# Graph layers on one core: six rows of z in step in place of five, other PSUM banks, row 5 of o in phase 2

## The reference, cut to what matters

```python
# layer 0
xw = x @ weight
Vxw = adj @ xw
scale = jnp.sum(d_list * filt * d_list, axis=0)
x = _layernorm(x + adj @ (scale[:, None] * Vxw) + bias)
# layer 1
X_in = (adj / where(rowsum(adj) > 0, rowsum(adj), 1)) @ x @ W_in
X_out = (adj.T / where(rowsum(adj.T) > 0, rowsum(adj.T), 1)) @ x @ W_out
out = _layernorm(x + X_in + X_out)
```

## Time and profile before

| | |
|---|---|
| median of 3 runs | 735.02 us (734.94 to 735.05) |
| the profiled execution | 734.96 us |
| its span | 733.1 us, so 1.9 us lie around it |
| PE busy | 726.4 us, 3293 matmuls |
| DVE busy | 598.0 us |
| ACT busy | 522.6 us |
| GpSimd busy | 18.6 us |
| DMA | 222.27 MB, mean 303 GB/s |

### The profile page before, as it was taken

One profiled execution on the slowest core, in us unless ns is written; L12 is line 12 of the kernel. 1 busy time (PEld: TensorE's weight loads), 2 busy tenths in 40 slices (PEclk: granted clock), 3 DMA queues, 4 the chain that ended last, 5 costly groups with the idle time before them and its releaser, 6 DMA issues.

```text
span 733.1 us, 9244 instructions
## 1 busy us (share of the span) xinstructions
PE 726.4 (99%) x3293; PEld 600.8 (82%) x3293; DVE 598.0 (82%) x754; ACT 522.6 (71%) x1336; POOL 18.6 (3%) x15
## 2 busy tenths in 40 slices
PE   9999999999999999999999999999999999999997
PEld 5888888888888888888888888888888888888885
DVE  6898997756363888998786778997898999899996
ACT  6888888737354639467374547998989898777673
POOL 1112400000000000000000000000000000000000
PEclk9999999999999999999999999999999999999999
DMA  9999999456443677666646469999989999999991
GB/s 371 426 425 423 425 427 387 173 179 229 173 173 118 226 266 307 232 268 247 230 175 266 157 213 390 381 386 389 367 325 391 385 368 379 379 362 352 357 367 34
DMA packets 36109, 222.27 MB, mean 303 GB/s; under 512 B 3680, under 2 KB 8544, under 8 KB 9568
## 3 DMA queue, kind: packets, MB, share of 16 engines
q1 hardware_dynamic: 35792, 221.56, 78.4%
q10 hardware_dynamic: 272, 0.13, 0.1%
HBM read 219.58 MB, written 2.10 MB: 302 GB/s over the span
## 4 chain that ended last, share of the span: by engine, by line
PE 99%; DVE 0%; ACT 0%; issue 0%; DVEq 0%; ACTq 0%
PE accA L716 13%; PE accA L721 13%; PE accB L716 13%; PE accB L721 13%; PE accA L726 13%; PE accB L726 13%; PE accC L721 6%; PE accC L716 6%; PE accC L726 6%; PE nat L775 3%; PE accB L821 1%; PE nat L782 0%; DVE stats L685 0%; ACT rows L428 0%; DVE accC L590 0%
## 5 line engine op out<-in xcount | busy, mean ns | idle before, releaser
L469 DVE TENSOR_TENSOR lo<-raw,hi 128x2048 fp32r<-128x2048 f32 (+2 forms) x249 | 476.1, 1937 | 86.0 <-ACT hi L325 74.8
L325 ACT ACTIVATE hi<-raw 128x512 fp32r<-128x512 f32 x512 | 315.4, 622 | 68.8 <-DMA raw<-in_adjT_b 42.4
L716 PE MATMUL accA<-hi,x_hi 128*128 128x512 f32 x416 | 163.3, 393 | 0.1
L721 PE MATMUL accA<-hi,x_lo 128*128 128x512 f32 x416 | 161.9, 389 | 0.0
L726 PE MATMUL accA<-lo,x_hi 128*128 128x512 f32 x416 | 116.4, 389 | 0.0
L716 PE MATMUL accB<-hi,v_hi 128*128 128x512 f32 x256 | 100.0, 391 | 0.0
L721 PE MATMUL accB<-hi,v_lo 128*128 128x512 f32 x256 | 99.6, 389 | 0.0
L330 ACT ACTIVATE hi<-raw 128x512 fp32r<-128x512 f32 x158 | 86.8, 621 | 17.2 <-DMA raw<-in_adjT_b 17.1
L325 ACT ACTIVATION_READ_ACCUMULATOR hi<-raw 128x1 f32 x512 | 97.6, 191 | 0.0
L716 PEld LDWEIGHTS accA<-hi,x_hi 128*128 128x128 f32 x416 | 78.2, 188 | 17.2 <-issue 1.2
L726 PEld LDWEIGHTS accA<-lo,x_hi 128*128 128x128 f32 x416 | 78.1, 188 | 16.3
(11 more groups left out here) (102 smaller groups left out, 502.1 us busy)
## 6 DMA issues: line engine op xcount, KB each, us to landing
raw<-in_adjT_b SPq DMA_DIRECT2D x143, 1024.0 KB, 5.8
raw<-in_adj_b SPq DMA_DIRECT2D x64, 1024.0 KB, 5.1
rows<-in_x_b SPq DMA_DIRECT2D x8, 256.0 KB, 9.6
out<-rows SPq DMA_DIRECT2D x7, 256.0 KB, 6.1
out<-rows SPq DMA_DIRECT2D x1, 128.0 KB, 1.8
out<-rows ACTq DMA_DIRECT2D x1, 128.0 KB, 2.1
coef<-in_coef_t SPq DMA_DIRECT2D x1, 96.0 KB, 9.0
w<-in_W SPq DMA_DIRECT2D x1, 64.0 KB, 9.0
```

The lines of the kernel that those rows point to most:

```text
L325: nc.scalar.activation(hi[slot][:, t], raw[slot][:, t], ACT.Copy, accum_out=to[:, TPB * K + t, C:C + 1]).then_inc(s_hi, 1)
L469: nc.vector.tensor_tensor(lo[slot][:, at], raw[slot][:, at], hi[slot][:, at], ALU.subtract).then_inc(s_lo, 1)
L716: nc.tensor.matmul(acc, r_hi[:, TPB * K + t], h[:, t], start=(first and t == 0), stop=False)
L721: nc.tensor.matmul(acc, r_lo[:, TPB * K + t], h[:, t], start=False, stop=False)
```

## The change

LEAD becomes 6: rows 0 to 5 of z run in step (n = 0 to 47), row 5 has no part of o in phase 1 and is treated in phase 2 as rows 0 to 4 are. z of rows 0 and 1 stands in accB, 2 and 3 in accA, 4 and 5 in accC, 6 and 7 in accA. Every row in step is turned four chunks past its last one: turn1 is 41, 43, 45, 47, 49, 51 for rows 0 to 5 and 57 for row 6. The bias is added behind every second chunk from 52 on, in place of every third from 44 on. Phase 2 has 49 chunks: 64 is (7,6), then (0,5), (7,5), (1,5), (2,5), (3,5), (4,5), (5,5), (6,5), then (0,4), (7,4), (1,4), (6,4), (2,4) and so on. o_sum(5) stands behind chunk 74, x1(5) behind 76. In all 213 chunks are loaded, not 207.

```diff
-LEAD = 5
+LEAD = 6
...
-    turn1 = {LEAD * NB - 4: 0}
-    for I in range(1, NB - 1):
-        turn1[LEAD * (NB - 1) + 4 + I if I < LEAD else last1[I] + 2] = I
+    turn1 = {last1[I] + (4 if I < LEAD else 2): I for I in range(NB - 1)}
     v_from = {n + 2: turn1[n] for n in turn1}
...
-        z_acc = [accA[:, 0], accA[:, 1], accC[:, 0], accC[:, 1], accB[:, 0], accB[:, 1]][:LEAD]
-        z_acc += [accA[:, (I - LEAD) % 2] for I in range(LEAD, NB)]
+        z_acc = [accB[:, 0], accB[:, 1], accA[:, 0], accA[:, 1], accC[:, 0], accC[:, 1], accA[:, 0], accA[:, 1]]
...
-                    if n == (N1 + 4 if I == NB - 1 else last2[I] + (5 if I >= NB - 3 else 4)):
+                    if n == (N1 + 4 if I == NB - 1 else last2[I] + (5 if I == NB - 2 else 4)):
                         deviation(NB - 1 - I)
...
-                if n >= 44 and (n - 44) % 3 == 0 and (n - 44) // 3 < NB:
-                    biased((n - 44) // 3)
+                if n >= LEAD * NB + 4 and n % 2 == 0 and n // 2 - LEAD * NB // 2 - 2 < NB:
+                    biased(n // 2 - LEAD * NB // 2 - 2)
...
-                    if n == last2[I] + (3 if I == NB - 3 else 2):
+                    if n == last2[I] + 2:
                         o_sum(I)
-                    if n == last2[I] + (5 if I == NB - 3 else 4):
+                    if n == last2[I] + 4:
                         x1_block(I)
                         x1_parts(I)
...
-                        pe.wait_ge(s_tz, I - 1 if I - 2 >= LEAD else I - LEAD + 1)
+                        pe.wait_ge(s_tz, I - LEAD + 3)
...
-                    if n == last2[I] + (3 if I == NB - 3 else 2):
+                    if n == last2[I] + 2:
                         turn_o(I)
```

## The result

The changed kernel takes 735.93 us (735.71 to 736.75, 22 runs), the kernel before 734.89 in the same comparison (734.73 to 735.28, 22 runs). The ratio is 1.0015, with a 95% interval of 1.0009 to 1.0021: about 1 us slower, less than the 0.2% (1.5 us) that the prediction took for the least that can be told. With 22 runs each the interval excludes the case of no change, though nearly all of it lies within 0.2%. The forecast was 735.7, with a range of 734.0 to 737.0.

What follows compares the result with a forecast made beforehand. The prediction took TensorE (PE), busy for 726.4 of 733.1 us, to bound the kernel. Its terms summed to 734.96 - 0.33 - 0.44 + 0.1 + 1.4 = 735.7 us, with a range of 734.0 to 737.0.

Steps and rivals of the forecast that it cites:

- The stall at chunk 77: Early phase 2: DVE has low(77) ready at 296.3, PE wants it at 294.9 in o77; +1.4 us.
- up to there both kernels do as much work: Starting point of the phase 2 count: o68 begins at 260.42 us, with equal work in both kernels before it.
- Chunk 69: Start of phase 2: low(69) is ready at 264.89, o69 wants it at 264.9; a stall of +0.1 us (0 to 0.3).
- The four transposes: Row 5 is no longer turned back by PE: four transposes and the longer matmul behind them go, -0.44 us.
- the first part's -0.33: Six rows in step, phase 1: without the x block ahead of it chunk 10 lands earlier, its PE gap goes; -0.33 us.
- I take no stall there: Chunk 12, which now has the x block ahead of it, causes no stall; bounds 0 and 0.33 us.
- Part 2 at no cost: Turning z rows four chunks past their end, new banks and later bias additions cost 0; bounds up to 0.5 and 0.3 us.
- a sign of being wrong: PE gaps at chunks 41 to 49, where v is made in step with the splits, would show the prediction wrong.
- Hidden: Rival: DVE is early enough at chunk 77 as its steps overlap more; only savings are left, 734.2 us; chance 0.33.
- The slower one: Rival: DVE's delay at o_sum(5) isn't won back between chunks 70 and 74; 1.9 us added, 737.6; chance 0.12.
- Doesn't save what it says: Rival: the gap at 34 us moves to chunk 12, a small stall eats the 0.44; 735.0 to 735.3 us; chance 0.05.

Runs made afterwards that it cites:

- e2: The changed kernel with x1(5) and its square root behind chunk 78 in place of 76: 734.80 us, ratio to before 0.9995.
- e11: The changed kernel with x1(5) behind chunk 77 in place of 76: 735.54 us.
- e4: The changed kernel with row 5 of o turned by PE again, DVE only copying the bank: 735.20 us, ratio to before 1.0004.
- e5: The changed kernel with two unused 128x512 additions on DVE behind o_sum(5): 737.68 us, ratio to before 1.0038.
- e9: The changed kernel with ACT's square root for x1(5) behind the split of chunk 77 in place of 76: 736.08 us, ratio 1.0014.
- e6: The changed kernel with the old turn1 rule (row 0 at chunk 44, rows 1 to 5 at 47 to 51): 735.99 us, ratio 1.0023.
- e8: The changed kernel with z of rows 0 to 5 in the old order of banks: 736.14 us, ratio 1.0019.

## Why the prediction was right

**The stall at chunk 77** was the term that decided. Predicted +1.4, measured 1.35, at the matmul that was named. Its working held from o68 on. Its starting point was wrong, though: "up to there both kernels do as much work" forgets that the six o products of row 5 no longer stand ahead of o68, 6 x 2.72 = 16.3 us. In the changed kernel o68 begins at 244.26 where it stood at 260.42 before, so the gap is not at the 294.5 that the prediction gives for it. That moves both engines alike and changes no difference between them: with the shift of 16.16 the forecast's times of 279.0 for o_sum(5), 288.7 for x1(5) and 294.9 for the matmul that waits become 262.8, 272.5 and 278.7. The trace has 262.68, 272.32 and 278.87 (278.64 and one step). e2, e11 and e4 remove or shrink it as they should, e5 doubles it, e9 clears ACT. The time within the range says less: 734.0 to 737.0 would have held without any stall too (734.2). It is the place and the size of the gap that bear the mechanism out.

**Chunk 69** was to cost 0.1 and cost nothing. The prediction's own numbers, ready at 264.89 and wanted at 264.9, gave nothing either. low(69) ended at 248.73, and PE's ninth matmul of o69 stands at its usual distance.

```profile
248.70 0.39 PE L718 MATMUL accB<-hi,v_lo 128*128 128x512 f32 x1
248.93 0.86 PE L723 MATMUL accB<-lo,v_hi 128*128 128x512 f32 x3
```

**The four transposes** brought the 0.44 expected: e4, which has them, takes 0.4 more than e2, which hasn't, both without a gap at 77. The rule of the Trainium skill (VectorE: DVE Perf Modes, Rules for kernel authors), to turn 128x128 on TensorE, agrees with e4 for this row: 735.20 with PE against 735.93 with DVE. It doesn't agree with e2, in which DVE turns row 5 and the kernel takes 734.80 (the intervals of e2 and e4 overlap, but the difference is that of the transposes): where DVE has cover, the 0.44 of PE is what counts.

**One term was wrong: the first part's -0.33.** The step that failed is "I take no stall there", with its bounds of 0 and 0.33 for chunk 12. I followed the DMA only as far as the chunk's landing. But block 2 of x is also loaded just ahead of its own first chunk, and behind its landing stands a chain: ACT makes x_hi behind the split of chunk 11, then GpSimd takes 1.90 us for x_lo, and PE's second matmul needs it. The kernel before has the same chain, and there it was in time:

```profile
29.00 2.20 ACT L330 ACTIVATE hi<-raw 128x512 fp32r<-128x512 f32 x4 [0.26 <-DMA raw<-in_adjT_b]
...
31.19 0.39 PE L716 MATMUL accB<-hi,x_hi 128*128 128x512 f32 x1
...
31.79 1.90 POOL L437 TENSOR_TENSOR x_lo<-rows,x_hi 128x512 fp32r<-128x512 f32 x1 [13.46 <-ACT x_hi L383]
```

x_lo was ready at 33.69, and PE would have begun chunk 10 at 33.90 had it been in time (33.45 of the earlier trace rows and two steps). So nothing was hidden behind the gap at chunk 10. The place of the block is what differs. ACT began chunk 9, the last split ahead of x_hi, 2.2 us before PE began that chunk. In the changed kernel the last split ahead of x_hi is chunk 11's, and ACT began it only 1.3 us before PE, for it had just waited 1.62 for chunk 10:

```profile
28.92 2.20 ACT L327 ACTIVATE hi<-raw 128x512 fp32r<-128x512 f32 x4 [0.27 <-DMA raw<-in_adjT_b]
32.73 2.20 ACT L327 ACTIVATE hi<-raw 128x512 fp32r<-128x512 f32 x4 [1.62 <-DMA raw<-in_adjT_b]
35.21 2.19 ACT L327 ACTIVATE hi<-raw 128x512 fp32r<-128x512 f32 x4 [0.28 <-DMA raw<-in_adjT_b]
...
36.48 0.39 PE L713 MATMUL accC<-hi,x_hi 128*128 128x512 f32 x1
```

The part gained 0.33 and lost 0.64, so it was worth +0.31 and not -0.33. The missed 0.64, less the 0.1 of chunk 69, the 0.09 gained at the start and the 0.05 by which the stall at 77 was smaller, makes up the 0.4 by which the spans' difference (1.1) exceeds the forecast's (0.7). That the small errors point the other way is luck.

**Part 2 at no cost:** e6 and e8 show that the new turns and banks are free. The bias additions weren't tried alone; no gap stands on PE near any of them, nor at chunks 41 to 49, which the prediction named as a sign of being wrong.

**The rivals.** "Hidden" fell: DVE's steps don't overlap more than the rows before showed. The slower one didn't occur: DVE made five low halves in 11.10 us, 2.22 each, and not at the pace of the releases. "Doesn't save what it says" was right in one point, that the gap at 34 us goes and one comes at chunk 12. But it is larger than that rival took it, and a wait for x_lo, not for a chunk.

## What to carry to other kernels

If one engine is dense, write down the order of the next engine's work behind the stage that changes, with durations from the rows, and compare the two clocks at each operand; here the matmul that waits and the size of the stall at 77 came out of that to a tenth of a microsecond. To move a step by two places in the order can do more than to take work off the engine: x1(5) behind chunk 78 in place of 76 took away all of the 1.35 in the trace (1.1 of the medians), and e4, which took 4.5 us off DVE for the same, paid 0.44 on PE. When a load is moved, follow it to the last engine that touches it, and look how far ahead of the dense engine that chain runs at the new place: block 2 of x kept its chain and lost 0.9 us of its lead.

## What the runs showed that I had not expected

A gap on PE costs about 0.1 us more than the wait itself: the step behind it is longer, 0.34 in place of 0.23 at chunk 12, and the four low matmuls behind the gap at 77 take 1.05 in place of 0.91. A subtraction of 128x512 takes 1.90 us on GpSimd (x_lo of phase 1) and 0.69 on DVE (x_lo of x1).
